# Several seams of a fused vision-transformer kernel reworked: value copies, router chain, variance order, last projection, FFN bias

## The chip, the cores and the metric

One program on one core of a Trainium2 chip. The metric is the device time of one execution in microseconds (us); lower is better. The profile comes from one profiled execution of the same program. Engines: PE is TensorE (PEld its weight loads), DVE VectorE, ACT ScalarE, POOL GpSimd, SP the engine that issues most transfers.

## The reference, cut to what matters

```python
h = patches(x) @ W_lin.T + b_lin, class token, + positions        # 16 images x 37 tokens, D = 256
h = h + attn0(layernorm(h))      # two sublayers inside: latent attention, then windowed grouped attention
h = h + moe(layernorm(h))        # 32 experts, top 8 in 2 of 4 groups, plus 2 shared units
h = h + attn1(layernorm(h))      # 16 heads, biases on qkv and on the output
h = h + ffn(layernorm(h))        # both products quantised per tensor

def _gate(x, gate_w, gate_bias):
    scores = sigmoid(x @ gate_w.T);  choice = scores + gate_bias
    group_scores = top_k(choice.reshape(T, 4, 8), 2)[0].sum(-1)
    keep the 2 best groups, masked = where(kept, choice, 0)
    topk_idx = top_k(masked, 8);  w = scores[topk_idx]
    return w / (w.sum(-1) + 1e-20) * 2.5

def _qlinear(x2d, w, b):
    xq, sx = _quant_per_tensor(x2d);  wq, sw = _quant_per_tensor(w)
    return (xq @ wq.T + b) * (sw * sx)
# ffn: o = _qlinear(gelu(_qlinear(x, w1, b1)), w2, b2)
```

## The kernel before

Activations are kept transposed: 256 features in two chunks of 128 partitions, 592 tokens (16 images of 37) along the free dimension in two halves of 296. Each engine has one program written out by hand, in order; counting semaphores (`s_...`) tie them together, and the order in an engine's program is the order of its work. PSUM is used as eight named banks, `ps[0]` to `ps[7]`.

**First attention block.** Two sublayers, a = 0 and a = 1. `qk_units(a)` makes queries and keys in six units (`QK_UNITS`, a half of the tokens each): PE projects, exchanges rows and sums squares, ACT copies and roots, DVE and POOL rotate and scale. The last unit's mean squares lie in bank 0, the one before in bank 1. The values of the first eight images are summed into bank 3 (`value_sums(a, 0)`) during unit 5, those of the other eight into bank 2 in the first steps of `attention(a)`. ACT copies both to `v4` (`values_copied(a, j)`, semaphore `s_v`): the first before the first `exponentials`, right behind the load of the Exp table. Then pairs of images follow: PE `scores`, ACT `exponentials`, PE `grouped_values` into bank `p % 2`, DVE `normalise_grouped` (a reciprocal and a product). PE's `grouped_values(a, 0)` waits for `s_v` and for the last unit's `s_qk`; DVE makes two of the four key variants of a half (line 966) when the unit behind it has been rotated. While this goes on POOL normalises the stream (a = 0, `layer_norm_stream`) or adds it to h (a = 1, line 501).

**Seam between the sublayers.** `stream_added` gives `x0` by halves, ACT squares it, PE sums (`stream_variance`), ACT takes the root (`stream_rsqrt`), DVE applies the norm. The second half's variance is summed behind the projections of units 0 and 1, and its root stands in ACT's program behind the copy and square of unit 1.

**Router and shared experts.** DVE first turns the FFN weights' peaks, which PE spread over bank 7, into scales (`scales_of(0, 2, 7, 1)`, `s_sc`); PE's second set of sums of shared unit 0 goes into banks 6 and 7 and waits for it. Then comes the router's chain on DVE: bias, top two of each group (20 MAX8), group sums, the groups' ranks by `gcmp` and `geq`, mask, top eight, weights, transposition. The products of the shared units' gates (`shared_product(n, j)`) are put between its steps: 0 behind the mask, 1 behind the match-replace, 2 and 3 at the end. Behind such a product ACT rounds, POOL subtracts and PE's `down_sums` follow. SP and ACT store the transposed weights, SP reads them back to all partitions (`wb`), and the first routed expert (unit 2) waits for that. From unit 4 on the experts run in a loop.

**Last attention and FFN.** `last_attention` ends with the projection of the second half of the tokens: PE seeds banks 4 and 5 with the centred stream through the identity matrix, sums the first half's variance, runs three matmuls that only keep it busy, waits for the last `s_on`, and adds the projection with 296 columns at once (`centred_projection(1, m, True)`); ACT squares it, PE sums, ACT and DVE normalise. In the FFN the hidden peaks are spread over bank 3; 18 busy matmuls bridge the time until the first quantised hidden chunk. At the end DVE scales b2, adds x0 (the plain projection), b2 and h in two instructions (line 1263), and then takes the four results out of banks 0 to 3 (line 1269).

## Time and profile before

| | us |
|---|---|
| median of 3 runs | 360.65 (360.07 to 361.62) |
| the profiled execution's own time | 360.19 |
| its span, first to last instruction | 358.4 |
| PE busy | 341.2 (95%) |
| DVE busy | 232.6 (65%) |
| ACT busy | 196.9 (55%) |
| POOL busy | 137.6 (38%) |

TensorE's mean granted clock is 0.999 of full speed. Read it so: the time is the span plus 1.8 us around it. PE's busy share includes matmuls that only keep it busy, and an engine's busy time says nothing of whether something waited for it; that is in the idle times, which stand in square brackets behind a row of the timeline with the engine that ended them.

### The profile page before, as it was taken

What the parts mean: (1) busy time and instruction counts of PE and PEld (TensorE: products, weight loads), DVE (VectorE), ACT (ScalarE), POOL (GpSimd) and SP (SyncE); (2) the same over time, 40 slices, a digit from 0 to 9 for tenths busy, and PEclk for the clock granted to TensorE, in tenths of its full rate; (3) what the DMA queues carried; (4) which work ended last, traced back from release to release, by engine and by line L of the source; (5) the groups of instructions that cost most, each with busy time, mean ns of one, the idle gap of its engine ahead of it and who ended that gap; (6) DMA issues with size and microseconds to landing.
All of it is one profiled execution on the core that took longest, in us unless ns stands there. A gap on an engine that the chain in (4) does not pass through costs nothing.

```text
span 358.4 us, 9932 instructions
## 1 busy us (share of the span) xinstructions
PE 341.2 (95%) x3931; PEld 292.8 (82%) x3931; DVE 232.6 (65%) x520; ACT 196.9 (55%) x400; POOL 137.6 (38%) x145
## 2 busy tenths in 40 slices
PE   8999889998988999999999999999999999999994
PEld 6866667676667989999999999999999678776662
DVE  3656788787879375555555555556557565666687
ACT  5367944787484335444444544544543786346772
POOL 0045761383160266555566544444440004241000
PEclk9999999999999999999999999999999999999999
DMA  8940000000560344455444445443410000000001
GB/s 284 405 159 1 3 5 7 24 3 5 171 182 3 96 115 137 145 156 155 138 122 148 137 154 155 137 135 136 143 27 2 0 0 4 6 4 3 2 0 68
DMA packets 14865, 32.08 MB, mean 90 GB/s; under 512 B 2480, under 2 KB 4464, under 8 KB 14576
## 3 DMA queue, kind: packets, MB, share of 16 engines
q1 hardware_dynamic: 13328, 30.48, 26.8%
q10 hardware_dynamic: 1504, 1.13, 0.9%
q8 instruction: 24, 0.39, 0.5%
q14 instruction: 9, 0.07, 0.1%
HBM read 30.91 MB, written 0.69 MB: 88 GB/s over the span
## 4 chain that ended last, share of the span: by engine, by line
PE 75%; DVE 10%; ACT 8%; issue 2%; DMA 1%; ACTq 1%; SPq 1%; POOL 1%; DVEq 0%
PE psum L1277 75%; DMA km<-in_experts 1%; DVE xn L907 1%; ACT region L861 1%; DVE nt L902 1%; ACTq L568 1%; DVE nt L904 1%; SPq L395 1%; ACT L589 1%; DVE km L1203 1%; ACT ah L746 1%; ACT region L681 1%; ACT e L693 1%; ACT sq L598 1%; DVE rt L1132 1%
## 5 line engine op out<-in xcount | busy, mean ns | idle before, releaser
L1277 PE MATMUL psum<-xh,split_all 128*128 128x296 f32 x544 | 121.5, 298 | 0.0
L506 POOL TENSOR_TENSOR split_all<-km,split_all 128x768 fp32r<-128x768 f32 x34 | 62.5, 1842 | 79.9 <-ACT split_all L725 79.9
L1277 PEld LDWEIGHTS psum<-xh,split_all 128*128 128x128 f32 x544 | 91.4, 188 | 0.1
L1277 PE MATMUL psum<-xl,split_all 128*128 128x296 f32 (+1 forms) x288 | 85.5, 301 | 0.3 <-POOL xl L549 0.3
L746 ACT ACTIVATE ah<-rt 128x296 fp32r<-128x296 f32 x64 | 28.9, 452 | 72.7 <-DVE rt L1132 66.0
L1277 PEld LDWEIGHTS psum<-xl,split_all 128*128 128x128 f32 (+1 forms) x288 | 53.3, 187 | 1.5 <-issue 1.1
L1277 PE MATMUL psum<-ah,split_all 128*128 128x296 f32 x272 | 48.5, 300 | 1.7 <-ACT ah L746 1.6
L1134 DVE TENSOR_TENSOR al<-rt,ah 128x296 fp32r<-128x296 f32 x60 | 28.0, 467 | 31.1 <-ACT ah L746 31.1
L1129 DVE TENSOR_TENSOR rb<-psum,wb 128x296 f32<-128x296 f32 x60 | 28.0, 467 | 24.4 <-ACT psum L744 24.4
L1277 PEld LDWEIGHTS psum<-ah,split_all 128*128 128x128 f32 x272 | 40.5, 189 | 2.6 <-ACT ah L746 2.1
L1132 DVE TENSOR_TENSOR rt<-rb,psum 128x296 f32<-128x296 f32 x60 | 27.8, 463 | 4.8
L744 ACT ACTIVATE psum<-psum 128x296 f32<-128x296 f32 x60 | 24.0, 399 | 11.1 <-PE psum L1277 11.1
L1277 PE MATMUL psum<-al,split_all 128*128 128x296 f32 x136 | 29.8, 300 | 0.2
L725 ACT ACTIVATE split_all<-km 128x768 fp32r<-128x768 f32 x34 | 28.3, 833 | 3.0 <-DMA km<-in_experts 2.9
L693 ACT ACTIVATE e<-psum 101x592 f32<-101x592 f32 x24 | 15.7, 664 | 22.6 <-PE psum L1277 22.4
L549 POOL TENSOR_TENSOR xl<-mx,cst 128x592 fp32r<-128x592 f32 x8 | 9.6, 1201 | 43.4 <-DVE mx L1212 43.4
L1277 PEld LDWEIGHTS psum<-al,split_all 128*128 128x128 f32 x136 | 21.9, 188 | 0.9 <-POOL al L512 0.5
L1277 PE MATMUL psum<-cstb 128*128 128x296 bf16 (+1 forms) x170 | 20.6, 297 | 0.3 <-DVE km L966 0.3
L977 DVE RECIPROCAL rc<-psum 128x148 f32<-128x148 f32 x16 | 17.3, 1083 | 5.3 <-PE psum L1277 4.1
L1277 PE MATMUL psum<-sq,cst 128*128 128x296 f32 x60 | 18.2, 417 | 0.5 <-ACT sq L598 0.5
L1277 PEld LDWEIGHTS psum<-cstb 128*128 128x128 bf16 (+1 forms) x170 | 12.0, 100 | 7.9 <-issue 4.4
L465 POOL TENSOR_TENSOR rt<-ra,rb 128x296 f32<-128x296 f32 x12 | 9.8, 821 | 14.9 <-DVE ra L949 14.9
(225 smaller groups left out, 582.0 us busy)
## 6 DMA issues: line engine op xcount, KB each, us to landing
km<-in_experts SPq DMA_DIRECT2D x34, 384.0 KB, 4.0
wb<-weights SPq DMA_DIRECT2D x32, 296.0 KB, 3.6
w_sb<-in_w SPq DMA_DIRECT2D x2, 1024.0 KB, 8.6
region<-in_x SPq DMA_DIRECT2D x6, 296.0 KB, 4.9
region<-in_w_lin ACTq DMA_DIRECT2D x6, 128.0 KB, 5.6
qkv_sb<-in_qkv_w SPq DMA_DIRECT2D x1, 768.0 KB, 4.9
cst<-in_consts SPq DMA_DIRECT2D x1, 502.5 KB, 7.0
out<-x SPq DMA_DIRECT2D x2, 148.0 KB, 1.8
```

The costliest lines, as they stand in the source:

```text
L465: nc.gpsimd.tensor_tensor(rt[:, u % 2, :], ra[:, u % 2, :], rb[:, u % 2, :], ALU.add)\
L506: nc.gpsimd.tensor_tensor(wl[i], ring[i], wh[i].bitcast(f32), ALU.subtract)\
L549: nc.gpsimd.tensor_tensor(dg[:, p % 2, :, :], mx[:, p % 2, :].unsqueeze(2).broadcast_to([P, HEADS, S]), const("minus_ident").unsqueeze(1). ...
L693: nc.scalar.activation(e[0:ROWS, p % 2, 0:EC].rearrange("p (k n) -> p k n", k=2), psum[0:ROWS, sb0:sb0 + 2, 0:HALFPOS * S], ACT.Exp, scale ...
L725: nc.scalar.activation(wh[i], ring[i], ACT.Copy).then_inc(s_wsh, 1)
L744: nc.scalar.activation(gate, ps[bank][:, 0:HALF], ACT.Silu).then_inc(s_sg, 1)
L746: nc.scalar.activation(ah[:, j, :], act[:, j, :], ACT.Copy).then_inc(s_ah, 1)
L977: link(nc.vector.reciprocal(rc[:], bank[:, G4 * S:2 * G4 * S]))
L1129: nc.vector.tensor_tensor(gu[:, j, :], gate, weight, ALU.mult).then_inc(s_mulc, 1)
L1132: nc.vector.tensor_tensor(act[:, j, :], gu[:, j, :], ps[5][:, 0:HALF], ALU.mult).then_inc(s_act, 1)
L1134: nc.vector.tensor_tensor(al[:, j, :], act[:, j, :], ah[:, j, :].bitcast(f32), ALU.subtract)\
L1277: return nc.tensor.matmul(out_, lhsT, rhs, start=start, stop=stop, skip_group_check=True)
```

## The change

- `first_values_copied(a)` on DVE, in the last pass of its `qk_units`, takes the first values out of bank 3 (`s_v0`); ACT keeps only the second copy. DVE's second pair of key variants moves behind the last unit. PE's first `grouped_values` waits for the first five units only, and the two banks change places (`1 - p % 2`), so that it writes bank 1; the second waits for all six.
- Between the sublayers PE sums the second half's variance before the projection of unit 1, and ACT takes its root before that unit's copies.
- Router: of the scales only the reading of bank 7 stays in front (`s_pkr`); the rest goes behind the transposition. Both comparisons lie in one tile `ahead` and are summed by one wider reduction, the test and the mask are one instruction, the factor 2.5 goes into the addition of 1e-20. Shared products 0, 1 and 2 stand sooner.
- Last projection: one seed before the last `weighted_values`; the second half is added in quarters of 148 columns, the first of which needs only pairs 4 and 5. The three busy matmuls go.
- FFN: b2 goes into banks 0 to 3 through the identity matrix, instead of 16 of the 18 busy matmuls; the peaks are spread over bank 4. POOL adds h to x0, by halves, as soon as the plain projection has been copied. DVE's three instructions go.

```diff
+            for hf in range(2):
+                pool.wait_ge(s_hn, hf + 1)
+                nc.gpsimd.tensor_tensor(x0[:, :, half(hf)], x0[:, :, half(hf)], h[:, :, half(hf)], ALU.add).then_inc(s_xh0, 1)
...
                 for u in range(NPROJ + 1):
                     n = a * NPROJ + u
+                    if a == 1 and u == 1:
+                        stream_rsqrt(1)
...
-                act_e.wait_ge(s_vz, 1)
-                values_copied(a, 0)
                 attention(a)
...
+                    if u == NPROJ:
+                        first_values_copied(a)
                     if u >= 1:
...
-                    if u >= 2 and QK_UNITS[u - 2][0] == 2:
+                    if u in (QK_UNITS.index((2, 0)) + 2, NPROJ):
...
+            def first_values_copied(a):
+
+                if a == 0:
+                    dve.wait_ge(s_vz, 1)
+                dve.wait_ge(s_vps, 2 * a + 1)
+                for g in range(2):
+                    rows = slice(64 * g, 64 * g + S)
+                    ins = nc.vector.tensor_copy(v4[rows, 0:HB, :, g, :],
+                                                ps[3][rows, :].rearrange("p (i h d) -> p i h d", i=HB, h=KVH))
+                ins.then_inc(s_v0, 1)
...
-                bank = ps[p % 2]
+                bank = ps[1 - p % 2]
...
-            scales_of(0, 2, 7, 1).then_inc(s_sc, 1)
+            dve.wait_ge(s_pkb, 1)
+            nc.vector.tensor_reduce(pk1[:, 0:2], ps[7][:, 0:2 * P].rearrange("p (n c) -> p n c", n=2), AX.X, ALU.max)\
+                .then_inc(s_pkr, 1)
...
+            own[0] += 1
+            ins.then_inc(s_dve, 1)
+            shared_product(0, 0)
+            dve.wait_ge(s_dve, own[0])
             link(nc.vector.tensor_tensor(gsum[:], top[:, :, :, 0], top[:, :, :, 1], ALU.add))
...
+            link(nc.vector.tensor_tensor(ahead[:, :, :, GROUPS:2 * GROUPS], others, mine, ALU.is_equal))
+            nc.vector.tensor_tensor(ahead[:, :, :, 0:GROUPS], others, mine, ALU.is_gt)
+            link(nc.vector.tensor_tensor(ahead[:, :, :, GROUPS:2 * GROUPS], ahead[:, :, :, GROUPS:2 * GROUPS],
+                                         bc(const("tie").rearrange("p (a b) -> p a b", a=GROUPS).unsqueeze(1),
+                                            [P, TT, GROUPS, GROUPS]), ALU.mult))
+            link(nc.vector.tensor_reduce(grank[:], ahead[:], AX.X, ALU.add))
+            link(nc.vector.scalar_tensor_tensor(
+                masked[:].rearrange("p t (g k) -> p (t g) k", g=GROUPS),
+                bc(grank[:].rearrange("p t g -> p (t g)").unsqueeze(2), [P, TT * GROUPS, PER_GROUP]), 2.0,
+                choice[:].rearrange("p t (g k) -> p (t g) k", g=GROUPS), ALU.is_lt, ALU.mult))
             link(nc.vector.tensor_scalar(masked[:], masked[:], 0.0, None, ALU.add))
...
+            shared_product(1, 1)
+            dve.wait_ge(s_dve, own[0])
...
+            nc.vector.tensor_reduce(wsum[:], wts[:], AX.X, ALU.add).then_inc(s_dve, 1)
+            shared_product(2, 0)
+            dve.wait_ge(s_dve, own[0])
+            link(nc.vector.tensor_scalar(wsum[:], wsum[:], 1e-20, 1.0 / ROUTED_SCALING, ALU.add, ALU.mult))
...
+            dve.wait_ge(s_pkr, 1)
+            link(nc.vector.tensor_scalar(scale[:, 0:2], pk1[:, 0:2], MIN_RANGE, 1.0 / QP, ALU.max, ALU.mult))
+            nc.vector.reciprocal(inv[:, 0:2], scale[:, 0:2]).then_inc(s_sc, 1)
             shared_product(3, 1)
...
-            link(nc.vector.tensor_scalar(b2s[:], vector("b2"), sxw[:, 1:2], None, ALU.mult))
-            dve.wait_ge(s_hn, 2)
-            for m in range(C):
-                ins = nc.vector.scalar_tensor_tensor(x0[:, m, :], x0[:, m, :], b2s[:, m:m + 1], h[:, m, :],
-                                                     ALU.add, ALU.add)
-            link(ins)
             for hf in range(2):
+                dve.wait_ge(s_xh0, hf + 1)
                 dve.wait_ge(s_f2, hf + 1)
...
                     if a == 0 and u < 2:
                         latent_sums(u)
+                    if a == 1 and u == 0:
+                        stream_variance(1)
                     if u + 1 < NPROJ:
                         projection(a, u + 1)
...
-                            pe.wait_ge(s_v, 2 * a + 1)
+                            pe.wait_ge(s_v0, a + 1)
+                            pe.wait_ge(s_qk, NPROJ * (a + 1) - 1)
+                        if p == 2:
                             pe.wait_ge(s_qk, NPROJ * (a + 1))
...
+            def add_projection(m, quarter):
+
+                for c in range(C):
+                    ins = mm(ps[4 + m][:, quarter * QUARTER:(quarter + 1) * QUARTER], outc_sb[:, c, m * P:(m + 1) * P],
+                             ot[:, c, HALF + quarter * QUARTER:HALF + (quarter + 1) * QUARTER], False, c == C - 1)
+                if quarter == 1:
+                    ins.then_inc(s_wc, 1)
...
+                    if p == PAIRS - 2:
+                        pe.wait_ge(s_mx, PAIRS)
+                        pe.wait_ge(s_cb, 2)
+                        seed_projection(0)
+
+                seed_projection(1)
+                pe.wait_ge(s_on, 3 * PAIRS - 2)
+                add_projection(0, 0)
                 pe.wait_ge(s_sq, 2 * C + 1)
                 for c in range(C):
                     ins = mm(ps[6][:, 0:HALF], const("mean"), sq2[:, c, :], c == 0, c == C - 1)
                 ins.then_inc(s_var, 1)
-                keep_busy(7, 3)
+                add_projection(1, 0)
                 pe.wait_ge(s_on, 3 * PAIRS)
                 for m in range(C):
-                    centred_projection(1, m, True)
+                    add_projection(m, 1)
...
-            peaks_spread(4, 2, 3, 6)
-            keep_busy(0, 18)
+            peaks_spread(4, 2, 4, 6)
+            for m in range(C):
+                for hf in range(2):
+                    mm(ps[2 * m + hf][:, 0:HALF], const("ident"), vector("b2")[:, m:m + 1].broadcast_to([P, HALF]), True, False)
+            keep_busy(5, 2)
```

## Rows read from the trace of the kernel before

**Rows 1.** Stretch: busy us of PE, PEld, DVE, ACT, POOL; clock; DMA share; GB/s.
```profile
131.00:269.00 138.00, 138.00 (x1022) 138.00 (x1022) 80.10 (x171) 66.53 (x143) 74.60 (x67) 1.00 0.44 134
```

**Rows 2.** Timeline, head of attention a = 0: start, length, engine, line.
```profile
41.02 1.21 DVE L966 TENSOR_SCALAR km<-sq,cst 128x296 f32<-128x296 f32 x2
41.93 1.18 ACT L681 ACTIVATE region<-psum 37x512 f32<-37x512 f32 x2
...
43.95 0.46 PE L1277 MATMUL psum<-e,region 101*32 101x74 f32 x16 [1.07 <-ACT e L693]
...
44.72 1.08 DVE L977 RECIPROCAL rc<-psum 128x148 f32<-128x148 f32 x1 [1.54 <-PE psum L1277]
```

**Rows 3.** Timeline, the same attention, pair 2 on DVE and pair 4 on PE.
```profile
47.78 1.08 DVE L977 RECIPROCAL rc<-psum 128x148 f32<-128x148 f32 x1
...
49.61 0.47 PE L1277 MATMUL psum<-e,region 101*32 101x74 f32 x16
```

**Rows 4.** Timeline, DVE reductions of 512 elements.
```profile
58.72 1.27 DVE L913 TENSOR_REDUCE pkp<-w_sb 128x1 f32<-128x512 f32 x2
```

**Rows 5.** Timeline, attention a = 1, head and last pair.
```profile
80.98 3.20 POOL L501 TENSOR_TENSOR h<-h,x 128x296 f32<-128x296 f32 x4
...
83.21 0.47 PE L1277 MATMUL psum<-e,region 101*32 101x74 f32 x16 [1.04 <-ACT e L693]
...
83.99 1.08 DVE L977 RECIPROCAL rc<-psum 128x148 f32<-128x148 f32 x1 [1.85 <-PE psum L1277]
...
93.23 0.47 PE L1277 MATMUL psum<-e,region 101*32 101x74 f32 x16 [0.43 <-DVE region L978]
```

**Rows 6.** Timeline, the seam between the sublayers.
```profile
67.65 0.78 DVE L907 TENSOR_TENSOR xn<-xn,nt 128x592 f32<-128x592 f32 x1
...
69.32 1.24 PE L1277 MATMUL psum<-xn,lk_sb 128*128 128x296 f32 x4 [0.80 <-DVE ra L949]
```

**Rows 7.** Timeline, router and shared experts.
```profile
109.82 1.46 DVE L1085 MAX8 top<-choice 128x8 f32<-128x8 f32 x20
...
110.62 0.40 ACT L744 ACTIVATE ra<-psum 128x296 f32<-128x296 f32 x1
...
114.35 0.57 PEld L1277 LDWEIGHTS psum<-ah,split_all 128*128 128x128 f32 x4 [1.40 <-ACT ah L746]
...
115.26 0.30 PEld L1277 LDWEIGHTS psum<-al,split_all 128*128 128x128 f32 x2 [0.33 <-POOL al L512]
...
118.97 1.34 ACTq L366 DMA_DIRECT2D weights<-wtr  x2
...
120.36 0.42 ACT L744 ACTIVATE ra<-psum 128x296 f32<-128x296 f32 x1 [0.94 <-issue]
...
122.38 0.71 PE L1277 MATMUL psum<-ah,split_all 128*128 128x296 f32 x4
...
125.66 0.84 DVE L1154 TENSOR_TENSOR rt<-psum,wb 128x296 f32<-128x296 f32 x2
```

**Rows 8.** Timeline, end of the last attention.
```profile
325.41 1.26 PE L1277 MATMUL psum<-xc,cst 128*128 128x296 f32 x4
...
327.89 2.15 PE L1277 MATMUL psum<-ot,w_sb 128*128 128x296 f32 x8
...
330.55 0.30 PEld L1277 LDWEIGHTS psum<-rs,cst 128*128 128x128 f32 x2 [0.48 <-ACT rs L849]
...
335.14 0.64 PE L1277 MATMUL psum<-cst,pk 128*128 128x128 f32 x4
```

**Rows 9.** Timeline, end of the FFN.
```profile
338.06 0.23 DVE L1237 TENSOR_SCALAR b1s<-vec,sxw 128x8 f32<-128x8 f32 x1
...
349.04 4.35 PE L1277 MATMUL psum<-km,w2q 128*128 128x296 bf16 x32
...
352.66 1.58 DVE L1263 SCALAR_TENSOR_TENSOR x<-x,b2s,h 128x592 f32<-128x592 f32 x2
354.27 1.83 DVE L1269 SCALAR_TENSOR_TENSOR x<-psum,sxw,x 128x296 f32<-128x296 f32 x4
```

More of the change, by code:

```diff
@@ L163, in program @@
         grank = sb("grank", [P, TT, GROUPS])
-        gcmp = sb("gcmp", [P, TT, GROUPS, GROUPS])
-        geq = sb("geq", [P, TT, GROUPS, GROUPS])
+        ahead = sb("ahead", [P, TT, GROUPS, 2 * GROUPS])
         wsum = sb("wsum", [P, TT])
@@ L285, in program @@
         s_v = sem("values_copied")
+        s_v0 = sem("first_values_of_an_attention_copied")
         s_s = sem("scores_summed")
@@ L652, in qk_units @@
                             .then_inc(s_qsq, 1)
-                    if a == 1 and u == 1:
-                        stream_rsqrt(1)
                     if u >= 1:
@@ L1106, in _ @@
                 ins = nc.vector.max(top[:, t, 0, :], masked[:, t, :])
-            link(ins)
+            own[0] += 1
+            ins.then_inc(s_dve, 1)
+            shared_product(1, 1)
+            dve.wait_ge(s_dve, own[0])
             for t in range(TT):
@@ L1477, in stream_variance, with centred_projection, seed_projection @@
                 ins.then_inc(s_var, 1)
-            def centred_projection(hf, m, seeded):
+            def centred_projection(m):
                 for c in range(C):
-                    ins = mm(ps[2 + 2 * hf + m][:, 0:HALF], outc_sb[:, c, m * P:(m + 1) * P], ot[:, c, half(hf)],
-                             c == 0 and not seeded, c == C - 1)
-                if m == C - 1 or hf == 1:
+                    ins = mm(ps[2 + m][:, 0:HALF], outc_sb[:, c, m * P:(m + 1) * P], ot[:, c, half(0)], c == 0, c == C - 1)
+                if m == C - 1:
+                    ins.then_inc(s_wc, 1)
+            def seed_projection(m):
+                mm(ps[4 + m][:, 0:HALF], const("ident"), xc[:, m, half(1)], True, False)
+            def add_projection(m, quarter):
[3 more added lines that the diff above has]
+                if quarter == 1:
                     ins.then_inc(s_wc, 1)
@@ L1574, in last_attention @@
                     if p % 2 == 0:
-                        pe.wait_ge(s_v, 4 + p // 2 + 1)
+                        pe.wait_ge(s_v, 2 + p // 2 + 1)
                     weighted_values(p)
-                pe.wait_ge(s_mx, PAIRS)
-                pe.wait_ge(s_cb, 2)
-                for m in range(C):
-                    mm(ps[4 + m][:, 0:HALF], const("ident"), xc[:, m, half(1)], True, False)
+                    if p == PAIRS - 2:
[5 more added lines that the diff above has]
+                add_projection(0, 0)
                 pe.wait_ge(s_sq, 2 * C + 1)
@@ L1812, in _ @@
                         ins = mm(ps[2 * m + hf][:, 0:HALF], w2q[:, ch, m * P:(m + 1) * P],
[L1813 removed]
+                                 hidq[:, ch, half(hf)], False, n == FC - 1)
                     if n == FC - 1:
```

58 lines of the change are left out of this document (20 added, 38 removed).

## The prediction

> **What bounds the kernel now.** I read the page's slices first, then the chain of waits, then the timeline around each edited place. Three quarters of the chain is PE, so the question at each edit is not whether an engine gets less work but whether PE, or a chain that PE waits for, starts sooner. The long expert loop is PE without a gap at the full granted clock [rows 1]: none of its time can be won, and whatever is won before it arrives behind it. In front of and behind it PE waits for others, and these waits are what the change touches.
>
> The reader is to see five of them. At the head of both attentions PE stands 1.07 and 1.04 us for an exponential that ACT makes only after copying the first values [rows 2, 5]. At the seam PE stands 0.80 us for the second half's norm [rows 6]. In the router the first `down_sums` waits 1.40 us, then 0.33 us more, for the shared activation [rows 7]. At the end of the last attention PE is nearly full [rows 8]. At the end of the FFN DVE runs two adds of 1.58 us after PE's last sums are almost done [rows 9].
>
> **First attention, a = 0: -0.5.** ACT loses one copy of values, two instructions, 1.18 us in all [rows 2]. PE, which waited 1.07 us, could start that much sooner, at 42.88. The two copies go to DVE, reading 512 elements per partition; the trace has no such DVE copy. From below the nearest row is ACT's own 1.18, from above 1.27 for two DVE reductions of 512 elements [rows 4]; I take 1.27, the same engine. Then on DVE: the copies take the place of the key variants (41.02 + 1.27 = 42.3), before PE is free at 42.88, so the new `s_v0` costs nothing; the last unit's two instructions took from 42.23 to 43.18 (DVE was idle 1.54 before 44.72) [rows 2], 0.95, now to 43.25; the variants follow, 1.21, to 44.45. DVE's first reciprocal starts there instead of at 44.72: only 0.27 sooner. From there DVE needs 1.53 us per pair (two pairs from 44.72 to 47.78), PE 1.415 (four pairs from 43.95 to 49.61) [rows 2, 3], and PE's pair k + 2 waits for DVE's pair k. DVE's pair 2 ends at 44.45 + 3 x 1.53 = 49.04, PE's pair 4 starts then instead of at 49.61: -0.5. After that PE runs on its own. So the saving is halved because the moved variants and copies make DVE the slower one. Bounds: -1.07 if the variants take half as long, +0.3 if they must wait for one more POOL instruction.
>
> One rule bears on this. Two variants of 296 elements took 1.21 us [rows 2], as long as two reductions of 512 [rows 4]; POOL was working on SBUF tiles beside them. The Trainium skill, SBUF — State Buffer, section "Who interferes with whom", says that VectorE in a two-port mode and GpSimd take turns on a shared port pair, the later to issue waiting for the whole other instruction; by it the variants can also wait for POOL's next instructions in their new place. The trace agrees, as far as the one long pair shows.
>
> **Seam: -0.8.** The second half's variance moves ahead of a projection of four matmul records, 1.24 us [rows 6]. ACT, DVE and the norm, which ended at 68.43, come about one us sooner, and with it DVE's first rotation. PE waited 0.80 us there, its queue before being the same work in another order, so 0.8 is what it can use. The stretch behind is PE in the chain, so it is kept. The two ACT instructions now stand ahead of unit 1's copy, 1 us; that copy is needed only after a projection which itself moved back, so nothing waits. Bounds -0.5 (unit 1's copy late) and -1.0.
>
> **Second attention, a = 1: -0.5.** The same edit. DVE was free at 83.99 - 1.85 = 82.14; POOL's four additions run from 80.98 to 84.18, 0.8 each, back to back [rows 5]. The two variants, now last, each get in behind one of them: 82.58 and 83.38, done at 83.55, so the first reciprocal comes 0.44 sooner. At the last pair PE already waited for DVE, 0.43 us [rows 5], so the end shifts by what DVE shifts, 0.4 to 0.6. SP's expert loads wait for the last scores and move by as much. They land in front of ACT's roundings, which stand before the next norm's squares, so these follow too. Bounds -0.96 (PE's waiting gone whole), +0.15.
>
> **Router: -1.2.** Two small instructions of the scales (0.37 us) leave the front, so the MAX8 group starts at about 109.5 and ends at 110.97; ACT's gate is ready at 110.62 + 0.40 = 111.02 [rows 7]. The product, until now behind seven more steps, runs 111.06 to 111.53, ACT rounds to 112.0, POOL subtracts 0.8 us to 112.9. PE's weight loads were ready at 114.35 - 1.40 = 112.95 [rows 7]: both waits (1.40 + 0.33 = 1.73) go. The next two products come in front of PE as well. DVE's chain loses an addition (0.25), a compare (0.2), a multiplication (0.2) and gains 0.1 in the wider reduction, and its products fill gaps: transposed at about 118.0. Then something is given back: ACT issues its stores behind that, 1.34 us, and its fourth gate stands behind them as now (0.94 idle, at 120.36) [rows 7], now from 119.4. Product, rounding and POOL give 120.85 and 121.75. PE would come to its fourth `down_sums` at 122.38 - 1.73 = 120.65 and waits 0.2, then 0.3 for the low part. That leaves -1.2. The routed expert's product at 125.66 [rows 7] needs the weights on all partitions; their stores end 1 us sooner than now, so they stay about hidden. The scales are now later, but POOL's first use is behind its low part of unit 4 at 125. Bounds -1.73, and -0.4 if the weights' transfer lets the routed product move by no more than that.
>
> **Last projection: -0.1.** PE's records of 296 columns take 0.27 us (eight in 2.15), those of 128 columns 0.16 (four in 0.64) [rows 8]. A quarter of 148 columns lies between; I take 0.16, nearest in width, 0.64 for four records. Behind the last `weighted_values`, 0.4 later now for the seed in front (its wait of 0.40 partly hid it), at 325.8: seed 0.53, quarter 0.64, mean 1.07, quarter 0.64 gives 328.68, later than today's 327.89. Then two quarters, to 329.96, and the mean's first chunk to 330.5, where the second chunk starts; it started at 330.55 [rows 8]. What the quarters save after the last `s_on`, 0.9, PE has spent before it. Bounds +0.2 (0.2 per record) and -0.5 (0.135).
>
> **FFN end: -1.1.** Removed on DVE: b2's scaling and 1.58 us of adds. PE's 32 matmuls end at 349.04 + 4.35 = 353.39, 0.136 each, the first half's sums two earlier, 353.12; DVE starts at 353.17 instead of 354.27 [rows 9]. Bounds -0.9 (start only at 353.39) and -1.3. On PE the four b2 matmuls are eight records of 0.27, 2.16 [rows 8], and two busy ones 0.27, against 18 x 0.136 = 2.45 [rows 9]: the same. POOL's two adds have nothing else on POOL and 14 us until they are wanted; if hidden no longer they would cost 1.5 each.
>
> Sum: -0.5 - 0.8 - 0.5 - 1.2 - 0.1 - 1.1 = -4.2. The profiled execution took 360.19, of which 358.4 is the span and 1.8 lies around it: 356.0. It lies 0.46 under the median of the three runs; against that it is 356.45. I give **356.2**.
>
> **Rivals.** *DVE takes over the attentions.* The variants fall behind more of POOL's instructions and both heads give nothing: 360.2 - 3.2 = 357.0, or up to 358.2 if they cost what the bounds and a third POOL instruction say. For it: the long pair and the 1.53 against 1.415; against it: the reciprocal starts sooner in my count in both. Chance 0.14. *The router's gain is given back* at the first routed expert, by the weights' transfer or ACT's stores: 0.3 left of 1.2, 356.9; together with the first 357.9. Chance 0.12. *POOL's add blocks DVE in the FFN.* b1's scaling is a DVE instruction at 338.06 [rows 9], and POOL's second add can start when ACT has copied the second half, some 0.2 us later; if it came first, the biases would wait for it and the first Gelu with them, 1.2 us: 357.2. By the rule named above this is what the later one suffers. Against it: that lead, which nothing here changes. Chance 0.04. *Slower: the expert loop settles in another phase.* It is entered with ACT's and POOL's work on the next expert standing differently to PE. If each of its 28 units made PE wait for the low part of the activation, x us each, it costs 28 x; above (4.2 + 1.8) / 28 = 0.22 the kernel is slower by over 0.5%, at 0.3 it is 364.4. Against it: PE waits nowhere in 138 us while DVE and ACT are busy 80 and 67 of them [rows 1]. Chance 0.02.
>
> **How the numbers follow.** My forecast, all six places within their bounds, has 0.68; its own range is 354.7 to 357.6. The bounds added up all one way would give 353.6 and 359.0; leaving one in ten on each side, and taking in the first rivals, the range is 354.0 to 358.4. About 0.5%, 1.8 us, is what a measurement of this kernel can tell from no change: slower than 358.85 needs two rivals at once. Faster 0.93, the same 0.05, slower 0.02.
>
> **What would show it.** In the changed kernel: ACT's first exponential of each attention right behind the table load; DVE's first reciprocal 0.2 to 0.5 sooner, and later pairs of PE waiting for DVE; PE's wait of 0.80 at the seam gone; no wait before the first `down_sums`, a small one before the fourth; the last projection's mean at the same distance from the last exponential; DVE's first result 0.8 us after its last hidden chunk. I am wrong if quarters cost little more than half of a half, if copies from PSUM on DVE take much over 0.6 each, or if the granted clock falls below full speed anywhere.

## The result, and the profile after

The changed kernel takes 357.14 us (median of four runs, 355.60 to 358.51) against 361.02 (360.07 to 361.62) of the kernel before on the same chip: ratio 0.9903, with 95% between 0.9874 and 0.9932. The forecast was 356.2, and its range 354.0 to 358.4. Timed anew it was 357.33 (six runs, 354.99 to 359.66), ratio 0.9904 [0.9868, 0.9939]. It is about 1% faster, and its runs scatter over 3 to 4.7 us where those of the kernel before scatter over 1.3 to 2.9. The profiled execution is the slowest of its four: 358.51, span 356.6.

The table cuts the span at eleven points that every version has and gives the length of each stretch, so that a delay in one does not hide a gain in the next. The second and fourth columns are from `before_again` and `again`, second profiles of the same two kernels; the last is from `ring_early` (below). Each number is the difference of two start times in the timeline; the last row ends with the span.

| stretch, us | before | before, 2nd | after | after, 2nd | ring_early |
|---|---|---|---|---|---|
| start to the token norm's `h` | 15.92 | 15.93 | 16.07 | 15.99 | 15.79 |
| to the grouped projection, a = 0 | 38.34 | 37.92 | 37.76 | 37.43 | 37.17 |
| seam, to the norm's fourth unit | 15.06 | 15.07 | 14.10 | 14.09 | 14.10 |
| to the grouped projection, a = 1 | 24.56 | 24.56 | 24.06 | 24.01 | 24.46 |
| to the router's sigmoid | 15.02 | 14.35 | 16.05 | 14.90 | 14.29 |
| router, to the loop's first `down_sums` | 21.84 | 21.85 | 21.17 | 21.17 | 21.71 |
| expert loop | 148.67 | 149.65 | 149.65 | 149.67 | 149.65 |
| last attention | 39.52 | 39.92 | 39.52 | 39.64 | 39.52 |
| last projection, to the plain one | 12.22 | 12.23 | 11.91 | 11.91 | 11.90 |
| FFN, to its last product's start | 17.89 | 17.92 | 17.87 | 17.85 | 17.86 |
| to the first result | 5.23 | 5.23 | 4.28 | 4.29 | 4.29 |
| rest | 4.10 | 4.09 | 4.11 | 4.10 | 4.10 |

All six edited stretches are shorter, the seam, the last projection and the FFN's end by the same amount in both pairs. Two stretches in which nothing was edited, the one up to the router's sigmoid and the expert loop, are longer in the first pair of profiles, by 1.03 and 0.98, which is about why this pair differs by 1.7 us and the runs by about 3.5. The first of them is longer in the second pair too, by 0.55. The windows view of the loop (busy us and number of instructions of PE, PEld, DVE, ACT, POOL; granted clock; DMA share; GB/s) answers to [rows 1]: PE is as full as before, but 1,016 products lie in the 138 us where 1,022 did.

```profile
131.00:269.00 138.00, 138.00 (x1016) 138.00 (x1016) 79.44 (x170) 66.08 (x141) 73.61 (x67) 1.00 0.43 134
```

The timeline of the first attention's head and its later pairs, after, answers to [rows 2, 3]. PE's first outputs come 1.14 us sooner once the 0.15 of the later start is taken off, with no wait in front. DVE's reciprocal comes only 0.34 sooner (0.49 so counted): it makes the copies in 1.38, then the last unit, then the variants in 0.93, and from the reciprocal on it runs without idle through five pairs.

```profile
41.17 1.38 DVE L984 COPY region<-psum 37x512 f32<-37x512 f32 x2
42.96 0.47 PE L1298 MATMUL psum<-e,region 101*32 101x74 f32 x16
43.54 0.93 DVE L973 TENSOR_SCALAR km<-sq,cst 128x296 f32<-128x296 f32 x2
44.38 1.06 DVE L995 RECIPROCAL rc<-psum 128x148 f32<-128x148 f32 x1
...
49.08 0.46 PE L1298 MATMUL psum<-e,region 101*32 101x74 f32 x16
...
49.88 0.30 PE L1298 MATMUL psum<-qt,km 64*37 64x74 f32 x8
51.24 0.59 PE L1298 MATMUL psum<-qt,km 64*37 64x74 f32 x24 [1.07 <-issue]
```

The second attention's head, answering to [rows 5]. Here the two variants take 1.21, beside POOL's additions.

```profile
79.47 3.33 POOL L503 TENSOR_TENSOR h<-h,x 128x296 f32<-128x296 f32 x4
80.69 0.47 PE L1298 MATMUL psum<-e,region 101*32 101x74 f32 x16
80.93 1.21 DVE L973 TENSOR_SCALAR km<-sq,cst 128x296 f32<-128x296 f32 x2
82.06 1.07 DVE L995 RECIPROCAL rc<-psum 128x148 f32<-128x148 f32 x1
```

The seam, answering to [rows 6]: PE's wait is gone from the row of the fourth unit.

```profile
67.44 0.66 PE L1298 MATMUL psum<-sq,cst 128*128 128x296 f32 x2
67.93 1.21 PE L1298 MATMUL psum<-xn,lk_sb 128*128 128x296 f32 x4
```

The router and the shared experts, answering to [rows 7]. PE's first two `down_sums` find their data. What stands in front of the fourth is ACT's gate, behind 1.61 us of stores; the compare of L1134 took 0.72 where its like took 0.32 before (the row by itself, from the kernel before).

```profile
109.76 0.40 ACT L749 ACTIVATE ra<-psum 128x296 f32<-128x296 f32 x1
...
112.03 0.60 PEld L1298 LDWEIGHTS psum<-ah,split_all 128*128 128x128 f32 x4
112.58 0.33 PEld L1298 LDWEIGHTS psum<-al,split_all 128*128 128x128 f32 x2
...
114.14 0.82 POOL L514 TENSOR_TENSOR al<-rt,ah 128x296 fp32r<-128x296 f32 x1 [1.99 <-ACT ah L751]
114.42 0.72 DVE L1134 TENSOR_TENSOR repl<-repl,masked 128x160 f32<-128x160 f32 x1
...
117.30 1.61 ACTq L368 DMA_DIRECT2D weights<-wtr  x2
118.96 0.42 ACT L749 ACTIVATE ra<-psum 128x296 f32<-128x296 f32 x1 [2.25 <-issue]
...
120.41 0.81 PE L1298 MATMUL psum<-ah,split_all 128*128 128x296 f32 x4 [0.58 <-ACT ah L751]
121.30 0.54 PE L1298 MATMUL psum<-al,split_all 128*128 128x296 f32 x2
...
124.16 0.84 DVE L1180 TENSOR_TENSOR rt<-psum,wb 128x296 f32<-128x296 f32 x2
```

```profile
115.92 0.32 DVE L1112 TENSOR_TENSOR repl<-repl,masked 128x160 f32<-128x160 f32 x1
```

The last projection and the FFN's end, answering to [rows 8, 9]: twelve matmul records of 148 columns in 1.67 us, 0.139 each, and DVE's first result 0.10 before PE's last product ends (348.16 + 4.38).

```profile
326.00 0.67 PE L1298 MATMUL psum<-ot,w_sb 128*128 128x148 f32 x4
326.51 1.16 PE L1298 MATMUL psum<-sq,cst 128*128 128x296 f32 x4
327.50 1.67 PE L1298 MATMUL psum<-ot,w_sb 128*128 128x148 f32 x12
329.18 1.27 PE L1298 MATMUL psum<-rs,cst 128*128 128x296 f32 x4
...
345.89 2.17 PE L1298 MATMUL psum<-vec,cst 128*128 128x296 f32 x8
348.16 4.38 PE L1298 MATMUL psum<-km,w2q 128*128 128x296 bf16 x32
352.44 1.83 DVE L1290 SCALAR_TENSOR_TENSOR x<-psum,sxw,x 128x296 f32<-128x296 f32 x4 [0.81 <-PE psum L1298]
```

### The profile page after: what moved, and what is told of

Its sections match the earlier page's. It is cut to its first block, busy times and chain, and to the rows that moved or that the text cites. A ratio compares the mean times of both kernels' runs of the same rounds, so it can differ in the third digit from the quotient of the medians.

```text
span 356.6 us, 9923 instructions
## 1 busy us (share of the span) xinstructions
PE 341.3 (96%) x3928; PEld 293.9 (82%) x3928; DVE 233.0 (65%) x518; ACT 194.6 (55%) x396; POOL 140.3 (39%) x147
## 4 chain that ended last, share of the span: by engine, by line
PE 78%; DVE 10%; ACT 5%; issue 2%; DMA 2%; ACTq 1%; SPq 1%; POOL 1%; DVEq 0%
PE psum L1298 78%; DMA km<-in_experts 2%; DVE xn L912 1%; ACT region L866 1%; ACTq L573 1%; SPq L397 1%; DVE nt L907 1%; DVE nt L909 1%; DVE km L1229 1%; ACT ah L751 1%; ACT sq L603 1%; DVE rt L1158 1%; DVE rb L1155 0%; DVE rt L1098 0%; ACTq L368 0%
## 5 line engine op out<-in xcount | busy, mean ns | idle before, releaser
L1298 PE MATMUL psum<-cstb 128*128 128x296 bf16 (+1 forms) x151 | 18.0, 298 | 0.3 <-DVE km L973 0.3
L1298 PEld LDWEIGHTS psum<-cstb 128*128 128x128 bf16 (+1 forms) x151 | 10.2, 100 | 7.4 <-issue 4.9
L1298 PEld LDWEIGHTS psum<-sq,cst 128*128 128x128 f32 x60 | 10.8, 189 | 5.5 <-ACT sq L603 2.6
```

What stands on the lines that cost most here:

```text
L1298: return nc.tensor.matmul(out_, lhsT, rhs, start=start, stop=stop, skip_group_check=True)
```

## The experiments

**again** is the changed kernel as it is.

> The changed kernel, nothing altered, to see what repeats. In its first profile the fourth expert's transfer took 5.74 us after its issue where it took 4.91 before, which held up ACT's squares (PE idle 1.70 us before the squares' sums), and the expert loop took 139.15 us for the same 1020 matmul records that took 138.22 before. Theory A, both are variation from run to run: the loop comes back to 138.2 to 138.6 and the transfer to under 5.2, and the time is 3.5 to 4.5 us under the kernel before. Theory B, both belong to the change (the loop is entered in another phase, the transfers meet other traffic): 139.1 and 5.7 again, the time 1.7 to 2.5 us under it.

357.33 us, ratio 0.9904 [0.9868, 0.9939]. Its profile (span 355.1) is the fourth column of the table. Neither theory holds whole: the fourth expert's transfer took 4.39 us instead of 5.74 and the time is 3.7 us under the kernel before, as theory A has it, but the loop took 149.67 again, as theory B has it. `before_again` looks at the loop.

**seam_only** is the kernel before with the seam's part alone: `stream_variance(1)` ahead of the projection, `stream_rsqrt(1)` ahead of unit 1's copy.

```
+                    if a == 1 and u == 1:
+                        stream_rsqrt(1)
...
-                    if a == 1 and u == 1:
-                        stream_rsqrt(1)
...
+                    if a == 1 and u == 0:
+                        stream_variance(1)
                     if u + 1 < NPROJ:
                         projection(a, u + 1)
...
-                    if a == 1 and u == 0:
-                        pe.wait_ge(s_x0, 2 * C)
-                        stream_variance(1)
```

> The kernel before with one part of the change: the second half's variance and its root sooner. In the changed kernel the seam won 0.96 us. If the parts are independent, PE's third-unit projection comes 0.8 to 1.0 us sooner here too and all behind it up to the expert loads moves with it; the whole time falls by 0.8 to 1.0 if the loads follow the scores, by nothing if their landing does not follow.

359.60 (ten runs), ratio 0.9958 [0.9941, 0.9974], so 0.9 to 2.1 us, of which the expected 0.8 to 1.0 is the lower end; the profile says where in it: the seam's stretch is 14.10, 0.96 less, as in every profile with the edit. Its loop took 149.64 us although nothing there was touched.

**ring_early** changes what the expert loads wait for. The ring of four buffers moves from the start of the key tile to its end, where the first three lie on none of the keys that this attention reads; only the fourth lies on the last key variant and waits for the last scores.

```
-        ring = [ring_all[:, i * EW:(i + 1) * EW] for i in range(NRING)]
+        RING_AT = (2048 + EW, 2048 + 2 * EW, 2048 + 3 * EW, 2048)
+        ring = [ring_all[:, at:at + EW] for at in RING_AT]
...
-            sp.wait_ge(s_s, 2 * PAIRS)
             for i in range(NRING):
+                if i == NRING - 1:
+                    sp.wait_ge(s_s, 2 * PAIRS)
                 sp.dma_start(ring[i], experts[i, :, :]).then_inc(s_ring[i], 16)
```

> The four expert buffers lie at the end of the key tile, so that three of them are free during the first attention and are loaded some 30 us sooner; only the fourth waits for the last scores. If the expert loads bound the norm in front of the router (my reading), ACT's squares start right behind the centred stream, about 2.0 us sooner than in the changed kernel (1.7 to 2.2), and the time falls by as much. If the norm is bound by what stands beside it anyway, ACT's or POOL's work on the experts moved elsewhere, under 0.5 us.

355.77 (five runs, 355.55 to 356.80), ratio 0.9858 [0.9838, 0.9878]: below `again` by 0.46 points, 1.7 us give or take 1.5 (the half widths of both intervals, squared, added, rooted), and a scatter of 1.25 us instead of 4.7 (the five later kernels with this ring have 1.5 to 3.0). The rows show why the norm comes sooner. In the changed kernel's first profile ACT rounds an expert that landed late and only then squares, 2.37 us after DVE's `xc`; PE waits 1.70. In `again` the loads came in time and the squares start after 0.49. With the loads ahead, the roundings are long done and the squares wait for nothing but their operand, 0.50. Against the first profile that is 1.87 sooner, as expected (1.7 to 2.2); against `again` it is nothing.

After (first profile):

```profile
98.30 1.82 ACT L730 ACTIVATE split_all<-km 128x768 fp32r<-128x768 f32 x2 [0.69 <-DMA km<-in_experts]
100.02 1.45 ACT L603 ACTIVATE sq<-xc 128x296 f32<-128x296 f32 x4
100.51 1.76 PE L1298 MATMUL psum<-sq,cst 128*128 128x296 f32 x6 [1.70 <-ACT sq L603]
```

again:

```profile
95.92 1.78 ACT L730 ACTIVATE split_all<-km 128x768 fp32r<-128x768 f32 x2 [0.23 <-DMA km<-in_experts]
97.70 0.82 ACT L603 ACTIVATE sq<-xc 128x296 f32<-128x296 f32 x2
```

ring_early:

```profile
93.70 1.56 ACT L732 ACTIVATE split_all<-km 128x768 fp32r<-128x768 f32 x2
97.68 0.82 ACT L605 ACTIVATE sq<-xc 128x296 f32<-128x296 f32 x2 [2.42 <-DVE xc L901]
```

What `again` still loses behind that is POOL's doing: POOL's subtractions follow ACT's roundings, and a DVE product of the norm that runs beside the last of them takes 1.05 us where it takes 0.47 with POOL done (rows and reading in the last section).

From DVE's `xc` to the sigmoid it is 8.62 or 8.63 us in all seven profiles with this ring, and 8.67, 9.21, 9.34, 9.36, 9.54 and 10.39 in the six others, of either kernel. So the stretch was already uncertain by 0.7 us with the loads of the kernel before (8.67 to 9.36, three profiles, `seam_only`'s among them), and by 1.2 in the changed one (9.21 to 10.39, three profiles, `silu_first`'s among them). On average the ring saves 0.8 of it by the six profiles, 1.1 by the three of the changed one; that it saves 1.7, as the runs would have it, is within their uncertainty and not shown.

**silu_first** lets ACT compute the fourth shared gate before it issues the weights' stores.

```
+                    act_e.wait_ge(s_g, n + 1)
+                    nc.scalar.activation(sg[:, j, :], ps[4 + 2 * j][:, 0:HALF], ACT.Silu).then_inc(s_sg, 1)
+                    if n == 3:
                         act_e.wait_ge(s_wtr, 1)
                         for q in range(2, 4):
                             store_weights(act_e, q)
```

> ACT takes the fourth shared gate before it issues its two stores of the weights, not behind them. In the changed kernel PE waits 0.58 us for the rounding and about 0.35 for the low part before its fourth down sums, and ACT's 1.6 us of issues stand before that gate. If they are what gives the router's gain back, both waits go: 0.8 to 1.0 us less up to the expert loop. If instead the weights on all partitions bound the first routed expert, its product stays where it is and the gain is under 0.3 us.

356.03 (six runs), ratio 0.9854 [0.9828, 0.9881], which is 1.8 us under `again`, give or take 1.6. PE's waits for both parts of the fourth activation are gone, but its router stretch is 21.41, longer than `again`'s 21.17: in this execution the granted clock fell (last section) and the first `down_sums` came 5.71 us after the sigmoid instead of 4.13. From there to the loop it took 15.70 against 17.04. How much of that 1.34 is the edit can't be read from this pair, since the late start also gave the chain time; `ring_silu_av` has the edit without that fall.

**ring_act_values**, **ring_dve_bias** and **ring_old_router** undo one part each, on the base of `ring_early` because its times lie close. The first gives the copies back to ACT, the variants their old places and the outputs their old banks. The second:

```
-                    mm(ps[2 * m + hf][:, 0:HALF], const("ident"), vector("b2")[:, m:m + 1].broadcast_to([P, HALF]), True, False)
+            link(nc.vector.tensor_scalar(b2s[:], vector("b2"), sxw[:, 1:2], None, ALU.mult))
...
+                ins = nc.vector.scalar_tensor_tensor(x0[:, m, :], x0[:, m, :], b2s[:, m:m + 1], h[:, m, :],
+                                                     ALU.add, ALU.add)
```

The third puts the kernel before's text back between `shared_product` and `expert_unit`, and both scales ahead of it.

> This is ring_early with the part of the heads undone: ScalarE copies the first values again, VectorE makes the key variants at the old places, the banks of the outputs are exchanged back. ring_early is taken as the base because its times lie close together (355.55 to 356.80) and its expert loads give nothing back. Theory (the part is worth what two profiles showed, 0.58 and 0.47 us): span 354.8 + 1.05 = 355.8, time about 356.8, ratio to the kernel before 0.9887. Rival 'VectorE takes over the attentions', read to its end: the shorter head is paid back by VectorE, so undoing it costs nothing: 355.8, ratio 0.9858, and the last projection of either attention starts as long after its ninth unit as in ring_early.

358.03 (six runs), ratio 0.9907 [0.9876, 0.9938]: 0.49 points over `ring_early`, 1.8 us give or take 1.3 (worked out as above). The part is worth something, and the rival that it is paid back whole falls. The two stretches up to the projections are 0.68 and 0.39 longer than in `ring_early`, with PE's stops in both (last section). Its profile can't be compared as a whole: the granted clock fell in its router (22.11), and its loop took 148.66 (see `before_again`).

> ring_early with the part of the FFN's end undone: VectorE scales the second bias and adds bias and stream in front of the results, TensorE's clock keeper is 18 products again. Theory: the first result comes 0.95 us later after the last product, as in the kernel before (1.5 to 1.6 us between them instead of none), 356.7, ratio 0.9884. Rival 'the end waits for TensorE anyway': VectorE's two additions fit beside the products, 355.8, ratio 0.986.

357.73 (six runs), ratio 0.9905 [0.9879, 0.9930]: 1.7 us, give or take 1.2. In the profile the stretch to the first result is 5.22 again, 0.93 more, and the FFN in front of it is the same.

> ring_early with the router's chain of the kernel before: both scales ahead of the chain, seven more small operations on the chain's path, the shared products where they were. Theory: the part is worth the 0.84 us that two profiles showed, 356.6, ratio 0.9882; TensorE waits for the first and the second down product again, and the waits in front of the fourth (for ScalarE's stores) are shorter. Rival 'the router's gain is given back at the fourth down product': under 0.3 us, 355.8 to 356.1, ratio 0.986 to 0.987.

356.28 (six runs), ratio 0.9876 [0.9848, 0.9904]: 0.65 us, give or take 1.2, which decides nothing. The profile does: 21.82, as in the kernel before, with PE's wait of 1.16 back in front of the first `down_sums`, against 21.16 to 21.18 in five profiles with the new chain (and 21.71 in `ring_early`'s, where the third `down_sums` came late by 0.5). Both expectations of this run missed: the part is worth 0.66, more than the rival's 0.3 and less than 0.84.

**ring_act_variants** takes the second half's two key variants from DVE and gives them to ACT, behind its first and third exponential.

```
                     exponentials(a, p)
+                    if p in (0, 2):
+                        g = ACT_VARIANTS + p // 2
+                        ins = nc.scalar.activation(km[:, 0, g, half(1)], sq[:, 0, half(1)], ACT.Copy,
+                                                   scale=const("onehot4")[:, g:g + 1])
```

> ring_early, and ScalarE makes the two key variants of the second half that VectorE made between the copies of the values and the first reciprocal (0.93 and 1.21 us of VectorE), one after the first and one after the third exponential. Theory (VectorE, not TensorE, now sets when the first pairs are done): VectorE's first reciprocal comes 0.7 to 0.9 us sooner, the attentions end 0.4 to 0.5 us sooner each, 354.9, ratio 0.9833. Rival 'the exponentials set the pace': ScalarE's two copies delay the second and fourth exponential by about 0.5 us, and PE waits for them: 355.8 to 356.3, ratio 0.986 to 0.987.

355.61 (five runs, 354.59 to 356.10), ratio 0.9852 [0.9825, 0.9879], which is 0.2 us under `ring_early`, give or take 1.2; its profile's span is 352.6. DVE's first reciprocal comes 0.65 and 0.59 us sooner in the two attentions, a little less than expected. PE's way from the first outputs to the projection has to be read without its stops (last section). In a = 0 it is 9.61 with stops of 0.27, so 9.34 without; `ring_silu_av`, which has these variants too, has 9.60 without. In six profiles of the edit with DVE's variants (0 to 1.55 of stops; `ring_more_products` left out, whose extra products delay the first outputs by 0.5) it is 9.74 to 9.82 without: DVE holds PE up by 0.14 to 0.48. The 0.26 between the two profiles with ACT's variants, whose code is the same up to there, says how well the stops can be taken off. In a = 1 `ring_silu_av`, without a stop, has 10.68 where three profiles without a stop have 11.26: 0.58. PE waits for no exponential in either attention, so the rival falls. By the profiles the theory stands, at about its size; the time is 0.7 over the expected 354.9, and by the timed runs alone the part would be open.

**ring_silu_av** puts the three together.

> All three of the steps that the earlier runs point to in one kernel: expert loads started early (ring_early), ScalarE's fourth shared gate ahead of its stores (silu_first), ScalarE makes the two late key variants (ring_act_variants). Theory (they act at three places and add up): from the start of the router's sigmoid to the loop 20.4 to 20.6 us instead of the 21.16 of ring_act_variants, attentions as there, span 351.9, time 353.9 to 354.9, ratio 0.980 to 0.983. Rival 'the router's chain, not the fourth gate, sets the loop's start': the 0.6 us in front of the fourth down product come back in front of the fifth and sixth, 352.6 and 354.6 to 355.6, ratio 0.985.

355.07 (five runs, 354.51 to 356.17), ratio 0.9839 [0.9819, 0.9859]: the fastest version of this study, 0.65 points under the changed kernel, and its interval lies wholly below that one's. The router stretch is 20.25 (20.4 to 20.6 was expected), 0.91 less than in `ring_act_variants`: that is what the fourth gate behind the stores costs. It is one profile, but five without the edit agree within 0.02 in this stretch. The timed runs (0.5 us give or take 1.2 against `ring_act_variants`) don't decide it. The whole time is 0.2 over the expected 353.9 to 354.9 and so within the rival's; but the rival had the 0.6 us come back in the router, and they did not. What the span, 353.1, has over the expected 351.9 is mostly a start 0.43 us longer than in `ring_act_variants` and stops of PE of 1.06 instead of 0.27 in the first attention. What is late next is the routed weights themselves; of the other profiles only `silu_first` has this wait of DVE, 0.19 there.

```profile
120.97 0.84 DVE L1192 TENSOR_TENSOR rt<-psum,wb 128x296 f32<-128x296 f32 x2 [0.38 <-DMA wb<-weights]
```

**before_again** and **ring_more_products** are one profile each, of the kernel before unchanged and of `ring_early` with `keep_busy(2, ATTENTION_BUSY + 4)`.

> The kernel before, for a second look at its expert loop: 1,020 products in 138.20 us in its one profile, 139.12 to 139.14 in every other profile so far, one of them with the loop's surroundings exactly as before. If 138.20 was one execution's, the loop takes 139.1 here; if it belongs to the kernel before, 138.2.

The loop's stretch took 149.65, as in eleven of the thirteen profiles. The kernel before so has the loop at both speeds: the 148.67 is not the kernel's but that execution's, evenly faster by 0.7%. One more execution had it, that of `ring_act_values`, 148.66, with the loop's code unchanged. The windows view of `before_again`, then of `ring_act_values`:

```profile
131.00:269.00 138.00, 138.00 (x1016) 138.00 (x1015) 79.72 (x169) 66.05 (x142) 74.13 (x67) 1.00 0.43 134
```

```profile
131.00:269.00 138.00, 138.00 (x1023) 138.00 (x1022) 79.76 (x171) 66.18 (x142) 73.24 (x67) 1.00 0.45 133
```

So the 0.98 that the first pair of profiles shows as lost is not shown to be an effect of the change. Both fast loops came with the attentions' old head, in two of its four profiles against none of nine with the changed one; with so few, that can be chance. Why two executions were faster, at the same granted clock of 1.00, stays open.

> ring_early with four more of the clock keeper's products (128 x 128 by 296) in PE's instruction stream ahead of the first attention's first output; nothing depends on them. PE stopped for 0 to 1.07 us with nothing to wait for in nine of ten attention pairs of profiles, always inside a scores group, after its 8th product in the first attention. Theory (the stop sits at a place in the instruction stream, say where the next piece of code must have been fetched): with four instructions more ahead of it, it comes four products (or eight, if a product is two instructions) earlier in the same group or in the group before, when it comes. Rival (the stop belongs to the work, such as a bank or a memory that is busy then): it stays after the 8th product.

Its rows are in the last section: the stop comes four products earlier in both attentions, the theory's four, and the rival falls.

## Why the prediction was right, by its own steps

The total fell inside the range, 0.9 us over the forecast. Terms read from the profiles, the first and third with PE's stops left out, give -0.85 - 0.96 - 0.55 - 0.67 - 0.31 - 0.95 = -4.3 against the -4.2 forecast; the runs show -3.5, with 2.2 to 4.8 inside the wider interval. That the sum agrees to 0.1 is in part luck: the router's term was 0.5 too large, and those of the first attention and the last projection together 0.56 too small. The 0.8 between -4.3 and the runs lies within their interval; PE's stops and the stretch up to the router's sigmoid, 0.6 longer on average with the change (9.71 against 9.12 behind `xc`, three profiles each), may hold it, which is not shown.

**First attention: -0.5 forecast.** The mechanism was right in its details: PE's first outputs 1.14 sooner, the reciprocal 0.34 sooner, DVE's pace 1.53, PE's pair 4 at 49.08 where 49.04 was forecast. But the forecast stopped at pair 4 against [rows 3], where PE ran freely, and did not look at the stop of 0.91 us behind it. With stops taken off, the kernel before needs 9.40 to 9.59 to the projection (four profiles), 0.06 to 0.25 over the 9.34 of `ring_act_variants`, and the changed one 0.40 to 0.48 over it: the saving is 1.14 less 0.15 to 0.41, so about -0.85. The first pair of profiles shows -0.58: 1.14, less the 0.40 by which the way without stops grew (9.40 to 9.80), less the 0.16 by which the stop was longer after the change. On DVE the copies took 1.38 instead of 1.27, and the two variants, which the prediction took over at 1.21, took 0.93 in their new place. For the copies, the Trainium skill, VectorE: DVE Perf Modes, section "The TRN2 errata — SBUF-src ops pay a fixed extra latency per instruction", has 120 cycles and one for each element from PSUM at 0.96 GHz, which makes an estimate of 0.66 us for one and 1.32 for both; the trace agrees within 0.06.

**Seam: -0.8 forecast, -0.96 found**, in eleven profiles alike. The term was mis-sized by reading the idle time of the row. The group of two products in front of it lasts 0.66 us by the profile, which models its end, but where nothing waits the next group starts 0.50 after it; so a wait of 0.80 after the modelled end is one of 0.96 for the queue. The bound of -1.0 held it.

**Second attention: -0.5 forecast, -0.55 found** where PE made no stop.

**Router: -1.2 forecast, -0.67 found.** This is the term that was furthest off. PE's gains came: 1.33 before the first `down_sums`, 0.46 before the second (2.44 behind the first instead of 2.90), together the 1.73 that was forecast and a little more. "That leaves -1.2", after 0.5 given back at the fourth, was wrong: 0.66 is lost there and 0.44 behind it. The stores start 0.81 sooner, seen from the sigmoid, not 1 us, since the compare at 114.42, which they wait for, took 0.40 longer; they last 1.61 and not 1.34; and the low part of the fourth activation comes 0.89 behind the high one instead of 0.54. `ring_silu_av` shows it on the chip: with the gate ahead of the stores the fourth `down_sums` stands 7.48 us behind the first instead of 8.24, and the stretch is 0.91 shorter. The rival of a gain given back named the stores and put what is left at 0.3; 0.67 is left. On the compare, the Trainium skill's SBUF — State Buffer, section "Who interferes with whom", has a DVE instruction with two inputs in SBUF contend with a POOL instruction that reads SBUF, and the one that came later wait for the whole of the other. POOL's ran from 114.14 to 114.96, the compare was due at 114.42 and ended at 115.14, 0.18 behind POOL's end. The trace agrees, and so do thirteen other instructions of these traces (last section).

**Last projection: -0.1 forecast, -0.31 found.** A record of a quarter costs 0.139 and not 0.16; the bound of 0.135 gave -0.5. Here half the columns cost half the time (0.27 at 296).

**FFN's end: -1.1 forecast, -0.95 found.** DVE starts 0.10 before PE's last product ends, where 0.22 was forecast, and POOL's additions were hidden.

**What no term held:** the expert loads, +1.03 in the first pair of profiles. The prediction let them "move by as much", and they did; what it missed is that their landing was never certain, in either kernel (the fourth took 4.39 to 5.74 us from its issue), that ACT's rounding puts it in front of the squares, and that POOL's subtraction behind the rounding can hold up DVE. Its rival of the expert loop in another phase has no profile for it: the changed kernel's loop took 149.65 and 149.67, and the kernel before has had 149.65 too.

## What to carry to other kernels

When a chain is shortened, look at what its engine issues next: here ACT's two stores stood between the shortened chain and the next wait, and moving one gate ahead of them was worth more by the profiles (0.91 us) than the whole edit of the router (0.67). Compare versions stretch by stretch over several profiles, since one pair can hold a loss of 1 us that no edit explains. A buffer whose reload waits for a late reader makes a stretch scatter: by 0.7 to 1.2 us here, and by 0.01 once three of four buffers lay elsewhere. The whole time still scattered by 1.25 to 3.0 us.

## What the runs showed of the hardware

**PE stops at a place in its instruction stream.** In both attentions PE idles for 0 to 1.07 us, marked "issue", with its operands there, always inside a group of scores products. The first row of each pair is the piece before the stop. With the changed head of the attentions the stop comes behind the 8th product of its group in a = 0 and the 7th in a = 1, with the old head (four profiles) behind the 9th and the 8th; in two profiles a = 0 has a second stop, behind the 1st product of an earlier group (0.66 and 0.45). Changed kernel, a = 0: see the rows at 49.88 and 51.24 above, behind the 8th product. ring_early, a = 1:

```profile
88.14 0.30 PE L1300 MATMUL psum<-qt,km 64*37 64x74 f32 x7
89.49 0.61 PE L1300 MATMUL psum<-qt,km 64*37 64x74 f32 x25 [1.05 <-issue]
```

ring_more_products, with four of the clock keeper's products more in front:

```profile
49.47 0.29 PE L1300 MATMUL psum<-qt,km 64*37 64x74 f32 x4
49.95 0.71 PE L1300 MATMUL psum<-qt,km 64*37 64x74 f32 x28 [0.19 <-issue]
...
87.85 0.29 PE L1300 MATMUL psum<-qt,km 64*37 64x74 f32 x3
88.37 0.71 PE L1300 MATMUL psum<-qt,km 64*37 64x74 f32 x29 [0.23 <-issue]
```

The 8th became the 4th and the 7th the 3rd. So the stop belongs to the code's position, not to the work. Its length changes from one execution to the next, 0 to 1.55 us for the first attention in thirteen profiles, and adds to the time nearly one for one; it is part of why two runs of one kernel differ. That the instructions' own fetch causes it fits, but was only argued.

**A DVE instruction can wait for a POOL instruction that started before it.** DVE's product of the norm, with POOL's last subtraction (94.78 + 7.14 = 101.92) still running, in `again`:

```profile
94.78 7.14 POOL L508 TENSOR_TENSOR split_all<-km,split_all 128x768 fp32r<-128x768 f32 x4 [12.38 <-ACT split_all L730]
101.19 1.05 DVE L909 SCALAR_TENSOR_TENSOR nt<-nt,ars 128x296 f32<-128x296 f32 x1
```

and with POOL done by then (93.14 + 7.15 = 100.29), in `ring_early`:

```profile
93.14 7.15 POOL L510 TENSOR_TENSOR split_all<-km,split_all 128x768 fp32r<-128x768 f32 x4 [11.21 <-ACT split_all L732]
101.17 0.47 DVE L911 SCALAR_TENSOR_TENSOR nt<-nt,ars 128x296 f32<-128x296 f32 x1
```

In all five profiles in which this product starts before POOL's subtraction ends, it ends 0.32 or 0.33 us behind POOL's end, whether it started 0.18 or 0.81 before it; with POOL done it takes 0.47. The router's compare takes 0.32 alone (four profiles) and 0.72 or 0.73 beside POOL (nine), and then ends 0.18 behind POOL's end. So 0.14 of the instruction's own time goes by during the wait, in both. Beside a POOL memset, which reads nothing, the same instruction, there in the first norm, took 0.47 (at 22.21 in the changed kernel).

**The granted clock can fall in the router.** In three of thirteen profiles, `silu_first`, `ring_act_values` and `before_again`, it was 0.50 to 0.70 for about four us of that stretch, where the others have 1.00. The windows view of `silu_first` and of `again`:

```profile
104.00:106.00 2.00, 1.40 (x13) 1.28 (x12) 1.89 (x4) 0.70 (x1) 0.00 (x0) 1.00 0.44 170
106.00:108.00 2.00, 2.00 (x13) 2.00 (x13) 1.88 (x13) 1.37 (x2) 0.00 (x0) 0.63 0.00 0
108.00:110.00 2.00, 2.00 (x9) 1.84 (x9) 1.02 (x13) 0.73 (x3) 0.00 (x0) 0.52 0.00 0
```

```profile
104.00:106.00 2.00, 1.40 (x14) 1.28 (x13) 1.89 (x3) 0.70 (x1) 0.00 (x0) 1.00 0.39 146
106.00:108.00 2.00, 2.00 (x17) 2.00 (x17) 1.89 (x16) 1.56 (x2) 0.00 (x0) 1.00 0.00 0
108.00:110.00 2.00, 2.00 (x13) 1.76 (x12) 1.90 (x15) 1.05 (x5) 0.39 (x1) 1.00 0.00 0
```

PE had been busy 1.40 of the 2 us in front in both, and only one fell, to 0.52, which is about the lower of the two levels (1.2 GHz of 2.4). In these three profiles the new router is the more exposed: the fall made the first `down_sums` late by 1.58 and 1.57 us there and only by 0.30 in the kernel before, where PE was waiting anyway, and the whole stretch longer by 0.94 in `ring_act_values` and not at all in `before_again`.
